# Cross-attention: who makes the low parts of the normalised rows and of the queries, Pool or DVE

## The reference: what is computed

```
ctx  = layernorm(context) * g + b
q    = layernorm(x) @ Wq ;  k, v = split(ctx @ Wkv)
sim  = einsum(q, k) * 64 ** -0.5        # 16 heads of 64
x    = x + softmax(sim) @ v @ Wo
```

## Time and profile before

| what | value |
|---|---|
| median of 3 runs | 2092.55 us (2091.82 to 2092.88) |
| the profiled execution | 2095.95 us, of which the span is 2094.2 us |
| busy share of the span | PE 90%, DVE 81%, ACT 57%, POOL 35% |
| `attend` | from about 105 us to about 1435 us of the span |
| one batch in the steady part | 81.5 us (from one wait at step 5 to the next, 519.46 to 600.98 us) |

### The profile page before, as it was taken

One profiled execution on the slowest core, in us unless ns is written; L12 is line 12 of the kernel. 1 busy time (PEld: TensorE's weight loads), 2 busy tenths in 40 slices (PEclk: granted clock), 3 DMA queues, 4 the chain that ended last, 5 costly groups with the idle time before them and its releaser, 6 DMA issues. The chain is left out here.

```text
span 2094.2 us, 33772 instructions
## 1 busy us (share of the span) xinstructions
PE 1876.3 (90%) x10010; PEld 1545.2 (74%) x10010; DVE 1689.0 (81%) x2835; ACT 1199.3 (57%) x2199; POOL 732.0 (35%) x416
## 2 busy tenths in 40 slices
PE   5889999999999999999999999997977578888885
PEld 4657777777777777777777777774854378888884
DVE  6668889888888898898898888885757568989973
ACT  3446667667667667666676666664533244544541
POOL 3022423423423324234234234120037444544443
PEclk9989999999999999999999999997999779999986
DMA  4821111111111111111111110006720355555522
GB/s 157 256 72 32 51 47 47 38 58 45 37 46 56 38 39 53 49 41 47 49 45 39 58 44 24 31 11 194 188 96 1 111 177 164 181 164 175 176 86 71
DMA packets 157493, 172.49 MB, mean 82 GB/s; under 512 B 12760, under 2 KB 124144, under 8 KB 157424
## 3 DMA queue, kind: packets, MB, share of 16 engines
q1 hardware_dynamic: 155888, 167.44, 25.4%
q0 software_dynamic: 1536, 4.20, 0.6%
HBM read 127.04 MB, written 44.56 MB: 82 GB/s over the span
## 5 line engine op out<-in xcount | busy, mean ns | idle before, releaser
L586 POOL TENSOR_TENSOR cl<-nrm,ch 128x255 fp32r<-128x255 f32 (+1 forms) x208 | 308.6, 1487 | 576.1 <-DVE ch L758 576.1
L684 ACT ACTIVATE s<-score 128x512 f32<-128x512 f32 (+1 forms) x416 | 248.8, 598 | 350.9 <-PE score L127 350.6
L717 DVE TENSOR_TENSOR s<-s,most 128x512 f32<-128x512 f32 (+1 forms) x416 | 322.4, 775 | 69.5 <-ACT most L660 69.5
L723 DVE TENSOR_TENSOR pl<-s,ph 128x512 fp32r<-128x512 f32 (+1 forms) x416 | 358.0, 861 | 0.7 <-ACT ph L666 0.7
L125 PE MATMUL acc<-ph,cl 128*128 128x512 f32 (+1 forms) x832 | 342.3, 411 | 1.4 <-DVE pl L723 1.4
L125 PE MATMUL score<-qsh,tl 128*128 128x512 f32 (+1 forms) x832 | 338.7, 407 | 0.8 <-DVE tl L752 0.8
L127 PE MATMUL score<-qsh,th 128*128 128x512 f32 (+1 forms) x832 | 327.0, 393 | 0.0
L126 PE MATMUL score<-qsl,th 128*128 128x512 f32 (+1 forms) x832 | 326.7, 393 | 0.0
L127 PE MATMUL acc<-ph,ch 128*128 128x512 f32 (+1 forms) x832 | 325.9, 392 | 0.0
L126 PE MATMUL acc<-pl,ch 128*128 128x512 f32 (+1 forms) x832 | 325.6, 391 | 0.0
L735 DVE TENSOR_TENSOR top<-top,s 128x512 f32<-128x512 f32 (+1 forms) x352 | 250.5, 712 | 18.5 <-ACT s L684 18.3
(11 more groups left out here) (257 smaller groups left out, 3687.8 us busy)
## 6 DMA issues: line engine op xcount, KB each, us to landing
raw<-in_ctx_in SPq DMA_DIRECT2D x192, 128.0 KB, 2.0
wr<-in_W SPq DMA_DIRECT2D x45, 512.0 KB
queries_scratch<-stage SPq DMA_DIRECT2D x32, 512.0 KB, 4.1
qr<-queries_scratch SPq DMA_DIRECT2D x32, 512.0 KB, 3.7
outputs_scratch<-o SPq DMA_DIRECT2D x32, 512.0 KB, 2.6
at<-outputs_scratch SPq DMA_DIRECT2D x32, 512.0 KB, 7.2
wr<-in_Wg SPq DMA_DIRECT2D x15, 1024.0 KB
wr<-in_Wl SPq DMA_DIRECT2D x15, 1024.0 KB
```

The costliest lines, as they stand in the source:

```text
L586: pool.tensor_tensor(cl[0:rows(t), t, 1:DIM], nrm[0:rows(t), t, 1:DIM], ch[0:rows(t), t, 1:DIM].bitcast(F32), ALU.subtract).then_inc(r_low, 1)
L684: act.activation(s[0:n, u, t, :], score[0:n, slot(0, u, t) % 2, :], ACT.Copy).then_inc(copied, 1)
L717: v.tensor_tensor(s[0:n, u, t, :], s[0:n, u, t, :], most[0:n, u, :], ALU.subtract).then_inc(shifted, 1)
L723: v.tensor_tensor(pl[0:n, ring(t), :], s[0:n, u, t, :], ph[0:n, ring(t), :].bitcast(F32), ALU.subtract).then_inc(p_low, 1)
```

## The change

POOL no longer makes the two low parts, and DVE makes them, with the same operands. The low part of the queries comes on DVE one step after the high part (steps 9 and 22; it stands behind `top` and before the statistics and `tl`). The low part `cl` of tile t comes one step after its high part, at steps 10, 11, 13, 15, 16, 18, 20, 21, 23, 25, 0, 2, 4; it stands behind `tl` and before the `ch` of that step.

```diff
-        at_rows = spread(LAG - KT + 1)
+        at_rows, at_rows_low = spread(LAG - KT + 1), spread(LAG - KT + 2)
...
@@ POOL's step
-                    if (f := k.unit(-5)):
-                        r, u = f
-                        pool.wait_ge(q_high, unit(r, u) + 1)
-                        pool.tensor_tensor(ql[:, u], qr[:, :, :], qh[:, u].bitcast(F32), ALU.subtract
-                                           ).then_inc(q_low, 1)
-                    for n, t in k.context(at_rows):
-                        pool.wait_ge(r_high, tile(n, t) + 1)
-                        pool.tensor_tensor(cl[0:rows(t), t, 1:DIM], nrm[0:rows(t), t, 1:DIM],
-                                           ch[0:rows(t), t, 1:DIM].bitcast(F32), ALU.subtract).then_inc(r_low, 1)
...
@@ DVE's step, behind the high part of the queries
+                    if (f := k.unit(-4)):
+                        r, u = f
+                        v.wait_ge(q_high, unit(r, u) + 1)
+                        v.tensor_tensor(ql[:, u], qr[:, :, :], qh[:, u].bitcast(F32), ALU.subtract).then_inc(q_low, 1)
...
@@ DVE's step, between tl and ch
+                    for n, t in k.context(at_rows_low):
+                        m = rows(t)
+                        v.wait_ge(r_high, tile(n, t) + 1)
+                        v.tensor_tensor(cl[0:m, t, 1:DIM], nrm[0:m, t, 1:DIM], ch[0:m, t, 1:DIM].bitcast(F32),
+                                        ALU.subtract).then_inc(r_low, 1)
```

## The result

The changed kernel takes 2100.48 us (median of 5 runs, 2097.71 to 2102.92) against 2092.55; the ratio is 1.0037, 95% interval 1.0023 to 1.0051: 0.4% slower. A second measurement of the same kernel gave 1.0038 (1.0025 to 1.0051). The forecast was 2103.0 us, range 2094 to 2109, slower with 74%.

A forecast was written before the change was run, and what follows sets the result against it. PE bounds the kernel, waiting for `tl` on DVE work after each release. Terms of +5.0, +4.7, +1.6 and -0.8 us sum to +10.5, so 2092.55 becomes 2103 us; range 2094 to 2109, slower with 74%.

The forecast's parts named there:

- PE sets the time, and loses it at steps 5 and 16, to `tl`: PE's transposes wait for DVE's `tl` twice a batch, losing 1.31 us at step 5 and 0.73 at step 16.
- Cost of `cl`, 0.33 us in the queue: One `cl` on DVE lasts about 0.41 us, overlaps 0.08 and delays DVE's queue by 0.33.
- the three places: Waits for `tl`: step 5, 15 times, +5.0 us; step 16, 14 times, +4.7; step 21, 14 times, +1.6.
- The first batch, -0.8 us: Before step 21 of the first batch, removed POOL disturbances outweigh the added low parts, saving 0.8 us in all.
- Sum, +10.5 us: 5.0 + 4.7 + 1.6 - 0.8 added to the kernel before, giving 2103 us, 0.5% slower.
- The long wait: PE's wait of 4.22 us for `tl` before step 21 of the first batch, with slowed matmuls behind it.
- The disturbance by POOL is worth nothing in the steady part: POOL's work stretches DVE instructions by 7.3 us a batch, but not in the runs before steps 5 and 16.
- The ledger of DVE as a whole: Faster rival: DVE's whole account, 7.3 us off and 6.6 on a batch, decides; 2083 us, at most down to 2064; 11%.
- The rival with the clock (2124 us, 4%): The wait before step 5 grows to 1.64 us and lowers PE's clock, 1.4 us each, 15 times; 4%.

The follow-up runs named there:

- rows only: Against the changed kernel, POOL keeps the low parts of the queries and only those of the rows move to DVE; 2102.87 us, ratio 1.0054.
- made twice: The changed kernel, with DVE making `cl` of row tiles 3 and 12 two times and waiting on the first; 2134.18 us, ratio 1.0196.
- thin POOL kernel: The kernel before, but POOL makes one column of each low part, the rest stay zero from fills at the start; 2091.93 us, ratio 1.0002.
- queries-only kernel: Against the changed kernel, POOL keeps `cl` and only the low part of the queries moves to DVE; 2093.8 us, ratio 1.0005.

## Why the prediction was right

- *PE sets the time, and loses it at steps 5 and 16, to `tl`.* Right, and shown from both sides: the losses grow with what stands between release and `tl` (full change, rows only, made twice), return when four instructions are moved behind `tl`, and vanish with `tl` at the head of the step, for 31 us of the attention stage.
- *Cost of `cl`, 0.33 us in the queue.* Right: 0.32 to 0.34 between starts, 411 ns long against 0.41 estimated. `ql` is 1215 ns long, 0.08 less is 1.14, as estimated.
- *+5.0, +4.7 and +1.6 us at the three places.* Right: the mean losses grew by 0.33, 0.33 and 0.13 us, or 5.0, 4.6 and 1.8. The batch grew by 0.82 us where these make 0.79, so that some 0.4 us in 14 batches isn't accounted for by them.
- *The first batch, -0.8 us.* From the first `turn` to the first wait at step 5 of the next batch it was 86.36 us (107.00 to 193.36) and is 85.80 (105.97 to 191.77), -0.56; with the 0.33 that this wait itself grew, -0.89. The long wait became 0.74 us shorter, and the clock still fell behind it.
- *Sum, +10.5 us.* The attention stage grew by 11.0. The time grew by 7.9, within the range and 2.6 below the forecast. The difference is in stages that the change doesn't touch: the forecast took them as unchanged, and they took 660 us beside 666 before. They are shorter where PE spends less time at its 1.2 GHz level, as the ten profiles show. The ten timed runs of the changed kernel have a granted clock of 0.952 to 0.957 over the whole span, the 38 fast runs of the kernel before that were timed beside the experiments 0.948 to 0.954. Why it was higher behind the changed stage is open, and the kernel with the low parts of the rows alone (+10.8 us in time, +9.4 in the stage) doesn't have that gap. That the time came out within 3 us of the forecast is thus in part luck, while the 11.0 us of the stage are not.
- *The disturbance by POOL is worth nothing in the steady part.* Right, shown by the batches of the thin POOL kernel (81.50 us in the mean, before 81.51). The ledger of DVE as a whole was the wrong account, as the queries-only kernel shows too: it relieves DVE and changes nothing.
- *The rival with the clock (2124 us, 4%).* It didn't happen in the change, but its mechanism exists and stood closer than I thought: at a recorded wait of 1.45 us the granted clock is 1.00 in the steady part, at 1.92 it fell in 10 of 14 batches. My price of 1.4 us each was about right (1.6). My forecast for the low parts made twice named it as a rival and left it out of the sum, which was 20 us too low.

## What to carry to other kernels

When two engines hand work back and forth, look for the event that releases the helper and the instruction that the leader waits for, and count only what stands between them in the helper's order; busy shares, and time given back to the helper elsewhere, said nothing about it here, and four instructions moved past that point cost nothing, on a helper that had idle time left. Before moving work from an idle engine to a busy one, ask whether the awaited instruction can go first in its step: here that was worth 1.6%, four times what the change cost, and made the choice of engine indifferent. A wait that recurs is priced at its length only as long as PE's clock stays up, so see what the granted clock does behind the longest wait of its kind in the trace.

## What the runs showed of the hardware

- A recorded PE wait of 1.91 to 1.92 us in otherwise dense matmuls was enough in 10 of 14 cases to bring PE to its 1.2 GHz level for some 3.4 us, and in the other four was not; the 14 waits of about 1.45 us (the longest 1.5) in each of three profiles never did in the steady part. The same wait thus costs 2.1 or 3.7 us. The first batch shows too that the length of a wait doesn't settle it: the clock fell behind 3.48 us in the changed kernel and stayed up behind 3.49 with the low parts of the rows alone, and it fell behind 2.96 us with four `cl` behind `tl` and stayed up behind 2.94 with thin low parts on POOL.
- POOL's part of the low parts stretches DVE's two-input instructions to nearly twice their length (1.23 beside 0.68 us), and none of the 7 us of that in a batch of the steady part reaches the end of the stage, as DVE waits anyway before the work that PE needs. What it costs in the first batch is not separated: the 4.4 us less with thin low parts on POOL come with a start of PE that is 3.7 us later.
